# Attention step of a decoder layer on five engines: another order of its operations, keys' projection and masked product in each other's banks

## The reference, cut to what matters

```
x = layernorm(x + linear_attention(x))    # relu(x Wqkv), 32 heads of 8; (v,1)^T k per head, then times q,
                                          # divided by the last row; projection, bias
x = layernorm(x + cross_attention(x, ctx))# 16 heads of 16; q and k rotated in float16 by two positions;
                                          # softmax(q k^T / 4) v; projection Wo, bias
x = layernorm(x + ffn(x))                 # x U1 V1 + b1, gelu, U2 V2 + b2; rank 64, 1024 wide
```

## Time and profile before

| | us |
|---|---|
| median of 3 runs | 553.57 (553.17 to 555.28) |
| profiled execution, its own time | 554.25 |
| its span, first to last instruction | 552.4 |
| mean granted clock of TensorE, share of full | 0.974 |
| the 15 attention steps | 61.0 to 448.4 |
| a middle step | 26.72 |

### The profile page before, as it was taken

One profiled execution on the slowest core, in us unless ns is written; L12 is line 12 of the kernel. 1 busy time (PEld: TensorE's weight loads), 2 busy tenths in 40 slices (PEclk: granted clock), 3 DMA queues, 4 the chain that ended last, 5 costly groups with the idle time before them and its releaser, 6 DMA issues.

```text
span 552.4 us, 11368 instructions
## 1 busy us (share of the span) xinstructions
PE 502.0 (91%) x4044; PEld 338.1 (61%) x4044; DVE 395.5 (72%) x878; ACT 316.5 (57%) x457; POOL 341.9 (62%) x391
## 2 busy tenths in 40 slices
PE   6997899899999999999999999999989678999992
PEld 3885566667676767676666667676745334545451
DVE  6567877787878778787878787878786676344454
ACT  3552366465657575656565656566656567656550
POOL 6659094858676776768585859594847324443425
PEclk9999799999999999999999999999989799999998
DMA  8654102202220313030203020401001001133332
GB/s 257 153 112 106 43 16 78 68 6 52 60 91 2 71 41 91 4 102 11 89 7 105 10 83 10 102 23 52 30 6 34 2 21 57 39 115 114 127 108 110
DMA packets 29131, 36.01 MB, mean 65 GB/s; under 512 B 5720, under 2 KB 15320, under 8 KB 29080
## 3 DMA queue, kind: packets, MB, share of 16 engines
q1 hardware_dynamic: 28216, 34.37, 21.4%
q10 hardware_dynamic: 864, 0.95, 0.8%
HBM read 23.51 MB, written 8.65 MB: 58 GB/s over the span
## 4 chain that ended last, share of the span: by engine, by line
PE 60%; DVE 15%; issue 13%; POOL 6%; ACT 5%; DMA 1%; POOLq 1%; SPq 0%; ACTq 0%
PE FR L1239 21%; PE BK L1413 9%; PE BK L1239 8%; DVE nmax L1036 5%; PE SC L1362 5%; PE FR L1322 3%; PE FR L1314 3%; PE SC L1394 3%; DVE lin_tm L946 2%; POOL rs L636 2%; PE FR L1441 2%; POOL c_fm L641 2%; PE SC L1239 2%; DVE rden L942 2%; DVE x_fm_l L1023 1%
## 5 line engine op out<-in xcount | busy, mean ns | idle before, releaser
L744 ACT ACTIVATE probs<-SC 128x1024 f32<-128x1024 f32 x128 | 130.6, 1024 | 97.3 <-PE SC L1394 97.3
L1036 DVE TENSOR_REDUCE nmax<-SC 128x4 f32<-128x1024 f32 x128 | 155.8, 1218 | 24.3 <-PE SC L1362 23.1
L1413 PE MATMUL BK<-probs,v_aug 128*32 128x256 f32 x1024 | 70.3, 393 | 0.0
L545 POOL TENSOR_TENSOR rs<-ve,minus_half 128x2 f32<-128x2 f32 x16 | 11.2, 700 | 85.9 <-DVE nm L1092 85.9
L1362 PE MATMUL SC<-k_blk,q_grp 48*128 48x512 f16 x256 | 51.9, 402 | 13.5 <-DVE nmax L1036 13.4
L850 ACT ACTIVATE probs<-SC,b_ff 128x512 f32<-128x512 f32 x64 | 38.8, 688 | 25.9 <-PE SC L1622 25.9
L1394 PE MATMUL SC<-q_grp,k_blk 64*128 64x256 f16 x512 | 50.1, 275 | 3.1 <-ACT q_grp L701 1.6
L1413 PEld LDWEIGHTS BK<-probs,v_aug 128*32 128x32 f32 x1024 | 27.0, 110 | 25.4 <-issue 14.6
L1394 PEld LDWEIGHTS SC<-q_grp,k_blk 64*128 64x128 f16 x512 | 25.2, 97 | 20.0 <-ACT probs L744 3.1
L1362 PEld LDWEIGHTS SC<-k_blk,q_grp 48*128 48x128 f16 x256 | 12.4, 93 | 39.5 <-DVE nmax L1036 20.4
L529 POOL TENSOR_TENSOR rs<-ve,minus_half 128x2 f32<-128x2 f32 x16 | 11.2, 700 | 37.4 <-DVE nm L1018 37.4
(11 more groups left out here) (239 smaller groups left out, 1500.7 us busy)
## 6 DMA issues: line engine op xcount, KB each, us to landing
x_fm<-in_x_fm SPq DMA_DIRECT2D x16, 256.0 KB, 5.7
x_tm<-in_x_tm SPq DMA_DIRECT2D x16, 256.0 KB, 5.3
x_kept<-x2b SPq DMA_DIRECT2D x16, 256.0 KB, 2.3
x_tm<-x_kept SPq DMA_DIRECT2D x16, 256.0 KB, 2.7
out<-c_fm SPq DMA_DIRECT2D x16, 256.0 KB, 2.0
c_fm<-in_c_fm SPq DMA_DIRECT2D x15, 256.0 KB, 6.3
tables<-rope_tables SPq DMA_DIRECT2D x16, 128.0 KB
k_blk<-k_rope SPq DMA_DIRECT2D x128, 16.0 KB, 1.8
```

The costliest lines, as they stand in the source:

```text
L744: act.activation(probs[:, j % 4], (SC[j % 2] if b == LAST else SB)[:], ACT.Exp, scale=SCALE).then_inc(s_exp, 1)
L1036: dve.tensor_reduce(nmax[:, t, :, 2 * q:2 * q + 2], src[:].rearrange("p (s f) t -> p s f t", s=2), AX.X, ALU.max, negate=True).then_inc(s_ ...
L1413: mm = pe.matmul(BK[q // 2][HP * k:HP * (k + 1), (q % 2) * T:(q % 2 + 1) * T], v_aug[b % NB][:, t, HC * q + k], probs[:, j % 4, k], start= ...
```

## The change

It reorders the calls inside `step` on all five engines; no arithmetic changes and no instruction is added or taken away. `k2` writes to FR[1] and `vk` to FR[0], each in the other's bank, and `lin(m, 1)` goes ahead of `lin(m, 0)`. `rope_k` and `rope_q` on GpSimd are each cut in two (the cosine product, and the rest), with other work between the halves; `norm1` on ScalarE is cut in its two activations. GpSimd's `split_x`, `keep_x2` and the queries' rotation go to later places, VectorE's `add1` goes behind `row_max(n1, 0)` and `ev_shift`, `q_halves` behind `lin` and `add2`. SP issues `place_q` before `keep`. The waits follow the banks.

```diff
@@ SP
-                if on(b - 2):
-                    keep(b - 2)
                 if on(b + 2):
                     place_q(b + 2)
+                if on(b - 2):
+                    keep(b - 2)
...
@@ GpSimd, step
+                if on(n):
+                    rstd1(n)
                 if on(q):
                     norm2(q)
                 if on(n):
-                    rstd1(n)
-                if on(m + 1):
-                    split_x(m + 1)
+                    rope_k_cos(n)
                 if on(p):
                     att_scale(p)
                 if on(n):
                     rope_k(n)
                 if on(p):
                     att_lo(p)
+                if on(n):
+                    rope_q_cos(n)
                 if on(m):
                     residual_bias(m)
+                if on(m + 1):
+                    split_x(m + 1)
+                if on(n):
+                    rope_q(n)
+                    residual2(n)
                 if on(q):
                     keep_x2(q)
-                if on(n):
-                    rope_q(n)
-                if on(n):
-                    residual2(n)
                 if on(m):
                     split_c(m)
...
```

The waits that change on TensorE and VectorE:

```diff
@@ k2
-                    pe.wait_ge(s_kv1_ev, 2 * (n + 1) + 2)
+                    pe.wait_ge(s_kv1_ev, 2 * (n + 1) + 1)
+                elif n >= 2:
+                    pe.wait_ge(s_proj_ev, B)
...
@@ x1_t
-                if n >= 2:
-                    pe.wait_ge(s_k2_ev, n + 1)
+                if on(n + 1) and n >= 2:
+                    pe.wait_ge(s_vk_ev, n + 2)
...
@@ x2_t
-                if on(q + 5):
-                    pe.wait_ge(s_vk_ev, q + 6)
-                elif q + 5 == B:
-                    pe.wait_ge(s_proj_ev, B)
+                if on(q + 4):
+                    pe.wait_ge(s_k2_ev, q + 5)
...
@@ lin on VectorE
+                dve.wait_ge(s_lin_mm, 2 * n + TT)
                 for t in range(TT):
-                    dve.wait_ge(s_lin_mm, 2 * n + t + 1)
```

More of the change, by code:

```diff
@@ L296, in build, with table @@
         block = ctx.enter_context(nc.Block())
+        def table(t, n):
+            return t[:, n * T:(n + 1) * T].unsqueeze(1).broadcast_to([P, CC, T])
         @block.sync
@@ L414, in _ @@
                     place_k(b + 2)
+                if on(b + 2):
+                    place_q(b + 2)
                 if on(b - 2):
                     keep(b - 2)
-                if on(b + 2):
-                    place_q(b + 2)
                 if b % 2 == 0 and on(b + 4):
@@ L477, in residual_bias, with rope_k_cos @@
                                    ALU.add).then_inc(s_xb, 1)
-            def rope_k(n):
-                cos, sin = (t[:, n * T:(n + 1) * T].unsqueeze(1).broadcast_to([P, CC, T]) for t in (cos_t, sin_t))
+            def rope_k_cos(n):
                 if n == 1:
@@ L609, in _ @@
             pool.wait_ge(s_q_rope, 1)
+            rope_k_cos(1)
             rope_k(1)
@@ L706, in ev_lint, with norm1 @@
                 act.activation(flat(lin_fm[0][:]), src[:], ACT.Copy).then_inc(s_lin_hi, 1)
[L708 to L714, removed]
+            def norm1(n, t):
+                if t == 0:
+                    act.wait_ge(s_mr1, n + 1)
+                    wait(act, s_x1b, n)
+                act.activation(x1_tm[:, t], y1[:, t], ACT.Identity, bias=mr1[:, t:t + 1],
+                               scale=rs1[:, t:t + 1]).then_inc(s_x1, 1)
             def ev_att(p):
@@ L808, in _ @@
             ev_q1(1)
-            norm1(0)
+            norm1(0, 0)
+            norm1(0, 1)
             ev_k2(1, SA0)
@@ L820, in _ @@
             ev_q1(2)
-            norm1(1)
+            norm1(1, 0)
+            norm1(1, 1)
             weights_hi(DD2)
@@ L1249, in q1 @@
             def q1(m):
+                pe.wait_ge(s_xs, m + 1)
                 if m >= 3:
@@ L1445, in step @@
                 n1, n, m, p, q = b + 1, b + 2, b + 3, b - 1, b - 2
-                if on(n1):
-                    scores1(n1, 0)
+                scores1(n1, 0)
                 if on(p):
                     scores2(p, 7)
-                if on(b):
-                    shift_t(b)
+                shift_t(b)
                 if on(m):
-                    kv1(m, 0, FR[1])
                     q1(m)
-                if on(n1):
-                    scores1(n1, 1)
-                if on(b):
-                    scores2(b, 0)
                 if on(p):
@@ L1463, in step @@
                     pv(p, 7)
+                scores2(b, 0)
+                scores1(n1, 1)
                 if on(m):
+                    kv1(m, 0, FR[1])
                     kv1(m, 1, FR[0])
-                if on(n1):
-                    scores1(n1, 2)
-                if on(b):
-                    scores2(b, 1)
+                scores1(n1, 2)
+                scores2(b, 1)
                 if on(n):
-                    k2(n)
-                if on(n1):
-                    scores1(n1, 3)
-                if on(b):
-                    scores2(b, 2)
-                    pv(b, 0)
-                    pv(b, 1)
+                    k2(n, FR[1])
+                scores1(n1, 3)
+                scores2(b, 2)
+                if on(m):
+                    vk(m, FR[0])
+                if on(q):
+                    x2_t(q)
+                pv(b, 0)
+                pv(b, 1)
+                scores2(b, 3)
+                scores1(n1, 4)
                 if on(n):
                     x1_t(n)
-                if on(m):
-                    vk(m)
-                if on(n1):
-                    scores1(n1, 4)
-                if on(b):
-                    scores2(b, 3)
-                if on(q):
-                    x2_t(q)
+                if on(q):
+                    p_ff(q)
+                pv(b, 2)
+                pv(b, 3)
+                scores1(n1, 5)
+                scores2(b, 4)
                 if on(n):
                     q2(n)
-                if on(q):
-                    p_ff(q)
+                scores2(b, 5)
+                scores1(n1, 6)
+                if on(m):
+                    lin(m, 1, FR[1])
+                    lin(m, 0, FR[0])
                 if on(p):
                     wo(p)
-                if on(n1):
-                    scores1(n1, 5)
-                if on(b):
-                    scores2(b, 4)
-                    pv(b, 2)
-                    pv(b, 3)
-                if on(m):
-                    lin(m, 0, FR[0])
-                    lin(m, 1, FR[1])
-                if on(n1):
-                    scores1(n1, 6)
-                if on(b):
-                    scores2(b, 5)
                 if on(n):
@@ L1515, in step @@
                     lin_t(m)
-                if on(n1):
-                    scores1(n1, 7)
-                if on(b):
-                    scores2(b, 6)
-                    pv(b, 4)
-                    pv(b, 5)
+                scores2(b, 6)
+                scores1(n1, 7)
+                pv(b, 4)
+                pv(b, 5)
                 if on(m):
```

123 lines of the change are left out of this document (54 added, 69 removed).

## The result

The changed kernel takes **563.69 us** (median of 4 runs, 562.13 to 565.77) against 553.75 (4 runs) for the kernel before, a ratio of 1.016 with an interval of 1.0135 to 1.0183. Its profiled execution took 563.59 us, with a span of 561.7 where the kernel before had 552.4.

What follows compares the result with a forecast made beforehand. TensorE was taken to bound the loop. Step changes of +9.2 us and clock falls of +3.2 made +12.4: 554.25+12.4-0.68 = 566.0 us, range 551 to 577.

Steps and rivals of the forecast that it cites:

- Part 1: TensorE's idle waits in a middle step removed: -1.15 us a step, to 25.55 if nothing takes their place.
- the four waits: TensorE's idle in a middle step: 0.34 before x2_t, 0.24 before k2, 0.31 before scores1(7), 0.11 before kv1(0).
- near approaches: Places in the new order with little time to spare, such as proj1 after lint; none to become a wait over 0.1.
- rival (d): The order doesn't remove the waits: a margin of 0.1 to 0.3 fails, costing 0.3 a step, +3; chance 0.05 alone.
- Part 2: GpSimd's order beside shift: residual2 at Q+9.1, shift at Q+9.2, so shift meets a busy GpSimd instead of an idle one.
- rival (a): Phase 0.1 us off, shift's first instruction before residual2: stall 1.4, step 26.95, total 555.7; chance 0.27.
- Part 3: Shift's three VectorE instructions held by GpSimd's: 3.1 us instead of 0.62, TensorE stall 2.0 us a step, bounds 0 to 3.2.
- Rival (b): Shift's three small instructions slip past GpSimd's unheld, 0.62 us in middle steps: -17, 536.6 us; chance 0.13.
- The clock term: Granted clock falls to half after TensorE stalls: two falls in the twelve steps, +3.2 us; bounds none and 19.
- rival (c): Clock falls in most steps: 6 to 12 falls of 1.6 on top of +9.2, 572 to 582 us; chance 0.12.
- The first steps: Step starting at 61.01: shift held about 1.6, +1.6 us; the second step +0.2.
- The end: Last two steps: row_max(0) ahead of add1 saves about 3, shift held once gives 2.0 back: -1.0 us.

## Why the prediction was right, point by point

I forecast 566.0 and measured was 563.69. The mechanism was right: which waits go, the phase, the three held instructions and their price in a middle step. That the total is so near is in part luck, as the table below shows. By its steps:

**Part 1, the waits removed: right in kind, low by 0.15.** The forecast step without the stall was 25.55; without holding it is 25.37 to 25.45. Every one of the four waits is gone. None of the near approaches (0.1 to 0.3 us) turned into a wait in a middle step, so rival (d) didn't occur.

**Part 2, the phase: right to 0.05 us.** Q, q2's first matmul, is at 236.45 in the kernel after. Forecast were residual2 at Q+9.1 and shift's first instruction at Q+9.2; they are at Q+9.14 and Q+9.24. The margin was small, but on the right side, so rival (a) didn't occur either. The kernel made to have it took 555.35, against the 555.7 named for it, with a stall of 1.55 for 1.4 and a step of 26.85 to 26.90 for 26.95. The near match of the totals is partly luck: beside its own kernel before it is +0.8, where +2.1 was named.

**Part 3, the holding: right in each of its three instructions.** Forecast were residual2, keep_x2 and the first half of split_c as the holders, 3.1 us for the three and a stall of 2.0. Measured: the same three holders, 3.04, and 1.92 idle. The doubtful third one is held too, 0.56 in the kernel after and 1.20 in the one with GpSimd later. The rule of the prediction, GpSimd's end plus the normal time less about 0.14, gives 0.04 to 0.05 behind, and so it was. So the Trainium skill (SBUF — State Buffer, "Who interferes with whom") is borne out for shift: the engine that starts second waits, tensor_scalar and, beside a GpSimd instruction that reads SBUF, instructions with two SBUF inputs are held, the reductions aren't (2.33 for two over SBUF in the kernel with two dummy ones). It also says there that an instruction with one SBUF input outside the two-port modes doesn't contend; with one operand in PSUM all three are indeed free (0.20, 0.19, 0.19), and so are the reciprocal and the shuffle above. The pair at 494.24 and the two instructions beside GpSimd's power are cases that it leaves unexplained.

**Rival (b), no holding,** didn't occur in the changed kernel, but its price was near: 536.6 for the kernel without holding, and the two that have none take 536.19 and 536.73. Its parts were off in opposite ways: in the kernel with nmax_c in PSUM the 13 steps before the last two gained 16.6, where 14.5 was named, and the last two 1.2, where 2.5 was.

**The sum by stages,** in the profiled executions:

| stretch | forecast | measured |
|---|---|---|
| first three steps | +2.6 | -1.35 |
| the next nine | +7.4 | +6.0 |
| the last full step | +0.2 | +0.7 |
| the last two, up to the last shift_t | -1.0 | +2.9 |
| falls of the clock in the twelve steps | +3.2 | 0 |
| ahead of the steps, and behind the last shift_t | 0 | +1.1 |
| all | +12.4 | +9.3 |

The first two rows and the clock came out 8.6 below the forecast, the other three 5.5 above it. Only the difference, 3.1, shows in the total, and that is luck.

**The clock term failed.** I had two falls from the wait of 2.04 that had one. In the kernel after none of the steps from 84.64 to 410.65 has any, with twelve waits of 0.91 to 1.92. The row of 1.47, which had none, was no better guide: in the kernel with two reductions a wait of 1.50 had a fall. So neither row could give the number of falls, and the runs don't either. In the three-reduction kernel every second wait of 2.75 to 2.77 was followed by a fall, so rival (c) names something that does occur, at a longer wait.

**The first steps were mis-sized.** I let keep_x2 take part in the second step, and I booked the first step's stall in that step. keep_x2 works on sequence b-2 and is absent in the first two steps. GpSimd's timeline of the kernel after at the second step's shift:

```profile
109.65 1.28 POOL L546 TENSOR_TENSOR x1b<-x_tm,b_o 128x512 f32<-128x512 f32 x1
110.90 0.63 POOL L465 TENSOR_SCALAR cs_fm_h<-c_fm 128x512 fp32r<-128x512 f32 x1
111.61 1.32 POOL L467 TENSOR_TENSOR cs_fm_l<-c_fm,cs_fm_h 128x512 fp32r<-128x512 f32 x1
```

and VectorE's:

```profile
109.76 1.21 DVE L1043 TENSOR_SCALAR nmax_c<-nmax 128x32 f32<-128x32 f32 x1
111.01 0.55 DVE L1047 TENSOR_SCALAR shift<-nmax_c 128x32 f16<-128x32 f32 x1
111.59 0.19 DVE L1049 SCALAR_TENSOR_TENSOR shift<-shift,nmax_c 128x32 f16<-128x32 f16 x1
```

Without keep_x2 the second instruction meets split_c's short half, and the third starts 0.02 ahead of the next one and is free. The waits are 1.19 and 0.91 rather than 1.6 and 2.0, and each lies in the window of the following step.

**The end was mis-sized, with the wrong sign.** Below, the last two steps of the kernel after, by windows (the last one up to shift_t), where before had 22.22 and 21.74, with shift_t at 449.0 (the earlier trace rows has the first):

```profile
410.65:434.71 24.06, 18.65 (x175) 11.92 (x175) 20.23 (x38) 14.11 (x19) 15.46 (x19) 0.93 0.07 20
434.71:457.50 22.79, 15.99 (x138) 7.31 (x138) 17.61 (x26) 11.32 (x14) 7.85 (x9) 0.78 0.08 27
```

I had counted on one held shift and on 3 us saved by row_max(0) ahead of add1. Two are held, with waits of 1.47 and 1.84, and two new waits of 0.56 stand behind them for the copy of the shifts into q_grp, beside one of 0.75 for GpSimd's rotated queries. TensorE's timeline of the kernel after:

```profile
434.71 0.39 PE L1349 MATMUL SC<-k_blk,q_grp 48*128 48x512 f16 x2 [0.75 <-POOL q_grp L512]
437.16 0.29 PE L1365 MATMUL FR<-ident,shift 128*128 128x128 f16 x2 [1.84 <-DVE shift L1049]
439.01 0.49 PE L1381 MATMUL SC<-q_grp,k_blk 64*128 64x256 f16 x4 [0.56 <-DVE q_grp L1054]
```

In the kernel with the clamped maxima in PSUM these two stretches take 22.53 and 20.19, 1.2 us less than before: the new order is worth 1.2 there, not 3, and the holding costs 4.1 on top: 3.3 of it is more idle time, and 0.8 is TensorE's longer busy time at a lower clock (0.78 against 0.83 in the second stretch). The exchange of the wait of 2.04 for one of 2.2 did come: it is 2.28 in that kernel, and 2.63 in the kernel after.

## What to carry to other kernels

Before work is moved on GpSimd, lay its timeline over VectorE's and mark VectorE's tensor_scalars, casts and instructions with two SBUF inputs whose operands all lie in SBUF: each of them, however small, can wait out a whole GpSimd instruction, and the chain of three small ones here waited out three. Reductions, reciprocals, shuffles and transposes were not held here. Where such a chain is on the path, keep one operand of each in PSUM or have GpSimd wait for the chain; either made this reordering a gain of 3.3% where it had been a loss of 1.6%. And where an order changed on several engines at once makes a kernel slower, look first for the one resource it collides with: the order itself may be good.

## What the runs showed of the hardware

- **Turns are taken instruction by instruction,** for the kinds of instruction that are held. A VectorE instruction of 0.18 us that starts 0.10 behind a GpSimd one ends 0.05 behind its end; GpSimd's next, already queued, then holds VectorE's next. Where VectorE started 0.02, 0.05 or 0.11 ahead of GpSimd's it was free (0.19, 0.18, 0.18), and GpSimd's instruction took at most 0.05 more (1.32 for 1.28 in the kernel after at 111.61).
- **A later GpSimd can make a faster kernel:** 0.15 us of added work on it in each step took off about 8 us, 6.8 of them in the steps.
- **The clock:** waits of 1.89 to 1.92 us in each of ten steps went with a granted clock of 1.00; waits of 2.75 to 2.77 went with a fall of 3.4 us in every second step, waits of 2.49 to 2.54 (GpSimd's old order) with one in three steps of four. One wait of 1.50 had a fall, and eleven of 1.63 to 1.64 had none.
